# Three matmuls with a tile of zeros as weights in each attention beat of a transformer layer, accumulated into the bank of PV

## The reference

```python
def proj(W, b):
    return (x @ W.T + b).reshape(B, S, H, hd).transpose(0, 2, 1, 3)
Q, K, V = (proj(Wq, bq), proj(Wk, bk), proj(Wv, bv))
scores = jnp.einsum('bhqd,bhkd->bhqk', Q, K) * scale
attn = jax.nn.softmax(scores, axis=-1)
out = jnp.einsum('bhqk,bhkd->bhqd', attn, V)
...
x = x + _L0_attn_ref(_layernorm(x, axis=-1), ...)
x = x + _L0_ffn_ref(_layernorm(x, axis=-1), ...)
```

## Time and profile before

| | us |
|---|---|
| median of 3 runs | 997.31 |
| lowest, highest | 993.49, 999.51 |
| the profiled execution | 992.53 |
| its span | 990.8 |
| mean granted TensorE clock in it | 0.69 |
| attention's first and last row maxima | 54.3, 713.2 |

### The profile page before, as it was taken

The page is one execution under the profiler, slowest core; times in us unless marked ns, Lnnn a source line. Parts: engine busy times, 40 slices in busy tenths (PEclk is TensorE's granted clock), DMA queues, the critical chain, the costliest instruction groups (busy, mean ns, idle before and its releaser), DMA issues. The chain is left out here.

```text
span 990.8 us, 13267 instructions
## 1 busy us (share of the span) xinstructions
PE 796.6 (80%) x3718; PEld 386.9 (39%) x3718; DVE 482.7 (49%) x1065; ACT 453.1 (46%) x943; POOL 255.7 (26%) x461
## 2 busy tenths in 40 slices
PE   4078999999999999999989988989894099899700
PEld 2044333333343343333324333433332098888700
DVE  3066447655446454645557545455512044444474
ACT  2035457644455445545446644544642054444322
POOL 4010010103020301212030140103105446555656
PEclk9997559756556555755658675555855599999955
DMA  1694104203201500320051032000000322222162
GB/s 51 91 255 69 20 1 84 27 22 68 43 1 33 93 6 1 78 53 2 22 95 15 23 78 31 1 1 23 1 1 22 97 61 63 61 65 63 55 183 72
DMA packets 50566, 50.25 MB, mean 51 GB/s; under 512 B 6782, under 2 KB 36010, under 8 KB 50484
## 3 DMA queue, kind: packets, MB, share of 16 engines
q1 hardware_dynamic: 44724, 39.99, 19.3%
q0 software_dynamic: 4416, 8.53, 2.5%
q10 hardware_dynamic: 1376, 1.13, 0.4%
HBM read 29.01 MB, written 20.61 MB: 50 GB/s over the span
## 5 line engine op out<-in xcount | busy, mean ns | idle before, releaser
L634 DVE TENSOR_REDUCE mneg<-s_psum 128x2 f32<-128x1024 f32 x256 | 309.6, 1223 | 283.7 <-PE s_psum L799 259.5
L541 ACT ACTIVATE pt<-st_psum 128x512 f32<-128x512 f32 x512 | 286.2, 596 | 300.4 <-PE st_psum L815 269.6
L873 PE MATMUL pv_psum<-pt,vst 128*32 128x512 f32 x1024 | 219.4, 948 | 0.0
L815 PE MATMUL st_psum<-qs,ks 32*128 32x512 f32 x512 | 182.0, 586 | 30.4 <-ACT pt L541 25.8
L799 PE MATMUL s_psum<-ks,qs 32*128 32x512 f32 x512 | 168.1, 698 | 30.8 <-DMA qs<-ks 27.7
L799 PEld LDWEIGHTS s_psum<-ks,qs 32*128 32x128 f32 x512 | 61.2, 251 | 231.5 <-DVE mneg L634 128.6
L815 PEld LDWEIGHTS st_psum<-qs,ks 32*128 32x128 f32 x512 | 89.1, 275 | 76.0 <-ACT pt L541 59.8
L1095 ACT ACTIVATE hid<-h_psum,b1c 128x256 f32<-128x256 f32 x144 | 57.1, 473 | 68.8 <-PE h_psum L1211 68.8
L1045 POOL DMA_INDIRECT results<-res,goal_now x72 | 71.6, 994 | 35.8 <-issue 35.8
L1218 PE MATMUL y_psum<-w2t,hid 128*128 128x128 f32 x576 | 71.8, 278 | 0.0
L1218 PEld LDWEIGHTS y_psum<-w2t,hid 128*128 128x128 f32 x576 | 68.0, 192 | 0.4
(11 more groups left out here) (161 smaller groups left out, 773.4 us busy)
## 6 DMA issues: line engine op xcount, KB each, us to landing
ks<-parts SPq DMA_DIRECT2D x96, 64.0 KB
qs<-parts SPq DMA_DIRECT2D x96, 64.0 KB
lot<-sent SPq DMA_DIRECT2D x37, 132.0 KB
parts<-high SPq DMA_DIRECT2D x16, 256.0 KB, 2.0
parts<-low SPq DMA_DIRECT2D x16, 256.0 KB, 2.3
got<-results SPq DMA_DIRECT2D x16, 256.0 KB, 3.3
xres<-in_L_attn_x_dram SPq DMA_DIRECT2D x8, 256.0 KB, 7.6
pt<-in_L_ffn_W_dram SPq DMA_DIRECT2D x1, 2048.0 KB, 22.3
```

The source lines that it names most:

```text
L541: nc.scalar.activation(pt[:, n % PT_SLOTS, g, :], st_psum[:, k % ST_BANKS, :], ACT.Exp, scale=SCALE).then_inc(exp_done, 1)
L634: nc.vector.tensor_reduce(mneg[:, (n // 4) % 2, at:at + 2], s_psum[:, k % S_BANKS:k % S_BANKS + 2, :], AX_X, ALU.max, negate=True).then_in ...
L815: mm(st_psum[:, k % ST_BANKS, :], ks[r, b % 2, c, P * (n % 4):P * (n % 4) + P], qs[r, b % 2, c, :], start=True, stop=True).then_inc(st_mad ...
L873: ins = mm(pv_psum[32 * g:32 * g + 32, 0, :], vst[:, b % 2, n % 4, 4 * (q % QUADS) + g, :], pt[:, n % PT_SLOTS, g, :], start=(n % 4 == 0), ...
```

## The change

A tile of zeros, 128 x 128 in float32r, is cleared by VectorE at the start, and TensorE's first use of constants waits for one more count. `values` calls the new `add_nothing(T)`: behind PV in the first block of a quad (where PV's `start` opens the accumulation), ahead of PV in the three others. It issues three matmuls with the zeros as weights and 512 columns of `w1h` as moving operand, added into all of `pv_psum`; in a beat with K, Q, V or O among its early tasks it issues one.

```diff
+        nothing = sb("nothing", [P, P], F32R)
...
+            nc.vector.memset(nothing[:].bitcast(U32), 0).then_inc(consts_ready, 1)
             nc.vector.memset(ones[:], 1.0).then_inc(consts_ready, 1)
...
-                pe.wait_ge(consts_ready, 1)
+                pe.wait_ge(consts_ready, 2)
...
                     pe.wait_ge(pv_copied, q)
+                if n % 4 > 0:
+                    add_nothing(T)
                 for g in range(4):
                     ins = mm(pv_psum[32 * g:32 * g + 32, 0, :], vst[:, b % 2, n % 4, 4 * (q % QUADS) + g, :],
                              pt[:, n % PT_SLOTS, g, :], start=(n % 4 == 0), stop=(n % 4 == 3))
                 ins.then_inc(pv_made, 1)
+                if n % 4 == 0:
+                    add_nothing(T)
+
+            def add_nothing(T):
+
+                heavy = any(kind in ("K", "Q", "V", "O") for kind, _ in early_tasks(T))
+                for _ in range(1 if heavy else 3):
+                    mm(pv_psum[:, 0, :], nothing[:], kept.w1h[:, 0:FC, :].rearrange("p c d -> p (c d)"),
+                       start=False, stop=False)
```

## The result

| | before | changed |
|---|---|---|
| median, us | 995.4 (4 runs, 981.8 to 999.5) | 1058.3 (4 runs, 1048.4 to 1064.1) |
| ratio, 95% interval | | 1.0705 (1.053 to 1.088) |
| profiled execution's span, us | 990.8 | 1056.5 |

The change makes the kernel 7% slower. The forecast was 959 us with a range of 910 to 1035, so the measured time lies outside it, on the other side.

The account below looks back on a forecast made before the run. TensorE, mostly at 1.2 GHz, was taken to bound attention. A 43 us gain in the beats less 5 us in the tail took 992.5 to 954.5 us; 4.8 us to the median gave 959, range 910 to 1035.

Parts of the forecast that it names:

- TensorE and its clock bound attention; the beats' lengths: Attention: TensorE is the bound, 78% of time at 1.2 GHz; light beats become 4.05 us at 2.4 GHz, 6.42 at 1.2.
- The formula: Period of 16 beats with additions: 70.7 us divided by (1 - share of time at 1.2 GHz x 0.37).
- What raises the clock: Attention beats: dense work over the whole array raises the clock, so every beat becomes a candidate for a rise.
- step 2: Price of one added 512-column matmul: 0.24 us at 2.4 GHz, bounds 0.21 and 0.32; three cost 0.72, or 1.44 at 1.2.
- The sign that the prediction had named for a wrong size: Profile after: a light beat at 2.4 GHz not near 4.05 us, or falls lying in plain light beats.
- step 5: Beats 8 to 127: share at 1.2 GHz falls to 25%, 4.87 us for each beat, gain 43 us.
- The falls: Clock drops where TensorE pauses: TURN behind LOGITS and COUNTS, X2T, standstills; a little over two in 16 beats.
- a sign of being wrong: Profile after: clock falls lying in plain light beats would show the forecast wrong on the size.
- raised but not held: Rival for attention's clock: share at 1.2 GHz 35 to 60%, 983 to 1056 us; chance 0.15.
- stated point of loss: Attention: at a share of 40% at 1.2 GHz, 83 us for 16 beats, the additions eat all the clock gives.

Follow-up runs that it names:

- the kernels with chosen places: Against the kernel before: five additions ahead of PV in two beats of 16, three waits filled, four behind PV in beat 0: 0.928; pieces moved to beats 1 and 9: 0.906.
- the thin matmul: Zero-weight matmul on 32 of 128 rows, away from PV in three of four beats, added to the changed kernel (1041.3 us) or to two additions per light beat (1053.0 us).
- The kernel with the additions apart: Changed kernel's 332 matmuls moved from PV to ahead of the second `scores_t` pair in three of four beats; 1075.6 us, 1.083 of the kernel before.

## Why the prediction was wrong

- *TensorE and its clock bound attention; the beats' lengths.* Right. The formula holds within 2%: with the share as measured, 0.62, and the forecast's prices, a period is 70.7 / (1 - 0.62 x 0.37) = 91.8 us, 5.74 for each beat, and with the measured prices 73.2 / (1 - 0.62 x 0.36) = 94.2 us, 5.89; measured 5.79.
- *What raises the clock: dense work over the whole array, zeros or not.* Right as far as the runs go: the share fell from 0.78 to 0.62, nonzero weights showed no advantage (a comparison between chips), and the kernels with chosen places use the rule to gain 7 and 9%. It is not shown that thin work does nothing: with the thin matmul the share rose in one kernel and fell in the other.
- *The price of an addition (step 2).* Mis-sized. Two, three and four lengthen a light beat at 2.4 GHz by 0.65, 0.88 and 1.12 us, one a heavy beat by 0.38: about 0.23 for each, and some 0.2 once for each piece. I put the 0.2 down to changing the array's shape, which no run isolates; the forecast took 0.24 for each with the shape in it. At 1.2 GHz three cost 6.55 - 4.98 = 1.57 us instead of 1.44. Alone the price at 2.4 GHz is 73.2 / (1 - 0.25 x 0.36) = 80.4 us for a period, 0.16 us for each beat of the 0.92 by which it missed. The sign that the prediction had named for a wrong size, a light beat not near 4.05 us, came too: 4.22.
- *The share of time at 1.2 GHz (step 5).* **This is the step that failed.** "A rise should now need one to two beats of 6.4 us, about 9 us" treats each beat as a new draw. It gave a share of 25%; measured were 62%, with stretches of 34 to 85 us, five to twelve beats of nearly one length. This is the other 0.76 us of each beat. I computed the beat's length at 1.2 GHz, 6.42 us, and did not ask what a fixed length does against decisions that come at their own times. The experiments with the thin matmul show that the beat's length has a large part in it: 0.60 to 0.42 by lengthening the beat of three on one chip, and 0.52 to 0.64 by lengthening that of two, across chips. The kernel with the additions apart (7.08 us, share 0.66) shows that it is not the length alone. The Trainium skill, TensorE: Matmul & The Clock Gate, section "What's actually happening", says that the chip's look at TensorE's activity runs freely and does not restart with the kernel. That a beat in step with it repeats its luck is my inference; the shares fit it, but no run shows the instants themselves. Had I drawn this before, the range of the share would have been far wider.
- *The falls.* Mostly right: in beats 1, 5, 15 and at the standstills of beats 8 and 9, and they go away where the wait is filled, though some come back at the next weak place. But three of the 14 falls of the changed kernel lie in beat 7, a plain light one, which I had called safer than before and had named as a sign of being wrong.
- *The rivals.* What came is the fourth, "raised but not held", just beyond its far edge (share 0.62 against 0.35 to 0.60, 1058 us against 983 to 1056); I gave it 0.15. Its stated point of loss, a share of 40%, is not tested at three additions at PV alone, whose share was never below 0.60; with the thin matmul beside them it came to 0.42, and the time was 4% over the kernel before (1041.3 and 999.3 us). Its neighbours lie around it: at 0.30 with four and at 0.52 with two, whose prices differ, the time is that of the kernel before.

## What to carry to other kernels

If TensorE is busy and its clock is low, dense work over the whole array at a few chosen places (a wait that is there anyway, where it can cost nothing, and directly behind places where the clock falls) was worth far more than a little in every step: here 0.906 against 1.07 of the time. The time at the low level did not follow the amount of added work, most likely because steps of equal length can fall in step with the clock's decisions. So test neighbouring amounts (two, three, four here) before believing one result in either direction, and judge by the share of time at each level, step by step, not by the mean.

## What the runs showed that I had not expected

- Matmuls with a tile of zeros as weights raise the clock, and no worse than those with 1e-30 as far as two chips can be compared: shares 0.60 to 0.64 and 0.58.
- A useless matmul of a quarter of the array did not lengthen the changed kernel's time (1041 against 1066 us, two runs each), although it made three of four beats at 1.2 GHz longer by 0.43 us; at 2.4 GHz a light beat did not grow at all.
- Chips differ: the kernel before takes 926.7 us on one (14 runs, mean clock about 0.745) and 991 to 999 us in the four other groups of runs (mean clock 0.67 to 0.69). Its beats were not profiled on the fast chip, so the reason stays open; the changed kernel was 1.05 to 1.07 of it on the others, and its twin with 1e-30 1.086 on that one.
